# A mixture-of-experts kernel: the gate weights move into the spare columns of the context chunks, and the early loads are merged

## The reference, cut to what matters

```python
x = x + tanh(g_xattn) * (gelu(layernorm(x) @ ctx.T) @ ctx)      # per batch, ctx is 375 x 256
n = layernorm(x)
top1 = argmax(n @ gate_w.T + gate_b)                            # 8 experts
x = x + tanh(g_ffn) * (relu(n @ w1[top1].T + b1[top1]) @ w2[top1].T + b2[top1])
```

## Time and profile before

| what | value |
|---|---|
| median of 3 runs | 111.12 us (110.9 to 111.33) |
| profiled execution, its time | 111.79 us |
| profiled execution, its span | 110.0 us |
| busy share of the span: TensorE | 92% |
| VectorE, ScalarE, GpSimd | 49%, 26%, 36% |
| mean DMA rate over the span | 258 GB/s |
| read from HBM | 26.33 MB |

### The profile page before, as it was taken

The page is one execution under the profiler, slowest core; times in us unless marked ns, Lnnn a source line. Parts: engine busy times, 40 slices in busy tenths (PEclk is TensorE's granted clock), DMA queues, the critical chain, the costliest instruction groups (busy, mean ns, idle before and its releaser), DMA issues.

```text
span 110.0 us, 2150 instructions
## 1 busy us (share of the span) xinstructions
PE 100.7 (92%) x704; PEld 92.7 (84%) x705; DVE 53.5 (49%) x204; ACT 28.6 (26%) x91; POOL 39.9 (36%) x97
## 2 busy tenths in 40 slices
PE   5999899999999997799999999999999999999900
PEld 5998669999988895799989999899999998998600
DVE  0461578669689884796555332344133241333010
ACT  5616143212351440152302303223032140220000
POOL 3276386353664937700330557030030030300330
PEclk9999999999999999999999999999999999999996
DMA  3999999999995202599999999999992010010101
GB/s 80 316 331 246 404 419 422 404 427 426 413 414 202 86 0 65 128 352 359 368 416 402 419 420 365 415 426 426 432 419 114 7 44 0 0 40 6 46 19 35
DMA packets 6734, 28.36 MB, mean 258 GB/s; under 512 B 1149, under 2 KB 2511, under 8 KB 4672
## 3 DMA queue, kind: packets, MB, share of 16 engines
q1 hardware_dynamic: 4688, 25.09, 58.2%
q0 software_dynamic: 864, 2.12, 6.3%
q10 hardware_dynamic: 1168, 0.98, 2.8%
HBM read 26.33 MB, written 2.11 MB: 259 GB/s over the span
## 4 chain that ended last, share of the span: by engine, by line
PE 71%; DMA 11%; DVE 6%; issue 3%; POOL 2%; SPq 2%; ACTq 0%; ACT 0%; POOLq 0%; DVEq 0%
PE bank L978 29%; PE bank L987 26%; DMA x<-in_x_rest 8%; PE bank L928 6%; PE bank L910 5%; DMA region<-x_rows,from_row 3%; PE bank L960 2%; PE bank L919 2%; DVE x L582 1%; SPq L241 1%; PE bank L900 1%; POOL out_rows L386 1%; DVE stats L589 1%; SPq L231 1%; DVE region L791 1%
## 5 line engine op out<-in xcount | busy, mean ns | idle before, releaser
L978 PE MATMUL bank<-region,w 128*128 128x128 f32 x288 | 34.7, 277 | 0.3 <-ACT region L485 0.3
L978 PEld LDWEIGHTS bank<-region,w 128*128 128x128 f32 x288 | 33.8, 192 | 0.8 <-ACT region L485 0.4
L987 PE MATMUL bank<-w,region 128*128 128x256 f32 x144 | 32.6, 379 | 0.0
L987 PEld LDWEIGHTS bank<-w,region 128*128 128x128 f32 x144 | 26.7, 190 | 3.2
L520 ACT ACTIVATE region<-bank,smalls 128x128 f32<-128x128 f32 x40 | 12.5, 363 | 39.9 <-PE bank L978 38.5
L386 POOL DMA_INDIRECT out_rows<-region,to_row x9 | 8.9, 989 | 33.9 <-DVE region L813 32.4
L797 DVE TENSOR_SCALAR region<-bank,smalls 128x128 f32<-128x128 f32 x32 | 9.7, 346 | 13.8 <-PE bank L978 13.4
L381 POOL DMA_INDIRECT region<-x_rows,from_row x9 | 9.3, 1032 | 15.7 <-DMA region<-x_rows,from_row 12.2
L813 DVE SCALAR_TENSOR_TENSOR region<-bank,tg,region 128x256 f32<-128x256 f32 (+1 forms) x9 | 4.4, 484 | 19.0 <-PE bank L987 19.0
L910 PEld LDWEIGHTS bank<-xnT,region 128*125 128x125 f32 x96 | 11.4, 188 | 2.2 <-issue 1.6
L910 PE MATMUL bank<-xnT,region 128*125 128x120 f32 x96 | 12.0, 275 | 0.8 <-issue 0.7
(11 more groups left out here) (118 smaller groups left out, 85.7 us busy)
## 6 DMA issues: line engine op xcount, KB each, us to landing
w<-in_w1t SPq DMA_DIRECT2D x8, 1024.0 KB, 23.3
w<-in_w2t SPq DMA_DIRECT2D x8, 1024.0 KB, 26.5
region<-in_ctx SPq DMA_DIRECT2D x5, 771.0 KB, 13.2
region<-in_ctx SPq DMA_DIRECT2D x3, 396.0 KB, 9.1
region<-in_ctx SPq DMA_DIRECT2D x3, 375.0 KB, 4.2
x_rows<-x ACTq DMA_DIRECT2D x8, 113.8 KB, 6.4
b2b<-in_b SPq DMA_DIRECT2D x1, 896.0 KB
x<-in_x_rest SPq DMA_DIRECT2D x1, 586.2 KB, 8.3
```

The lines of the kernel that those rows point to most:

```text
L978: mm = pe.matmul(hT_ps[k][:, part % 2 * P:(part % 2 + 1) * P], w1[:, e, n * H + part * P:n * H + (part + 1) * P], xgT[:, j % 2, n * P:(n + ...
L987: mm = pe.matmul(y[:, 0:D], hidT[:, q, part, :], w2[:, e, part * D:(part + 1) * D], start=(part == 0), stop=(part == KH - 1))
```

## The change

The gate weights leave `x_logits`. A chunk of context has 125 rows for 128 positions; its transposed form now gets 128 columns, and the three spare ones of each chunk hold gate weights, so the scores give x times gate weights in the output rows 125 to 127. ScalarE copies the last 32 output rows without gelu (`spare_rows`) before the gelu of the first 125 overwrites those of them that are context rows. The context rows get 8 more columns, with ones in the spare rows only, so `attend` carries the values past the gelu into columns 264 to 271. `x_share` therefore reads its input from attend's output. For the last batch VectorE does that itself in two small instructions (`add_last_logits`). `xnT` moves into the space of the last expert's w2. Contexts 0 and 1 come in two pieces (transposed, rows), x of batches 2 to 7 in one, contexts 2 to 7 whole, and w2 of expert 1 is loaded after SP's wait.

```diff
-DL = D + E
-CW = KD * CTX + CC * DL
+SPARE = P - CR
+CT = KD * CC * P
+DL = D + 2 * E
+CW = CT + CC * DL
...
-HEAD = 3
+HEAD = 2
...
-            load_x(0).then_inc(x_in[0], 16)
-            load_context_T(0)
-            load_x(1).then_inc(x_in[1], 16)
-            load_context_T(1)
-            load_x(2).then_inc(x_in[2], 16)
-            load_context_rows(0)
-            sp.dma_start(x2[0:S, HEAD:B, :], x_rest).then_inc(x_in[3], 16)
-            load_context_T(2)
-            load_context_rows(1)
-            load_context_rows(2)
-            for b in range(3, B):
-                load_context(b)
+            for b in range(HEAD):
+                load_x(b).then_inc(x_in[b], 16)
+            sp.dma_start(pair_T, ctx_pair[:, 0:HEAD * CT]).then_inc(pair_T_in, 16)
+            sp.dma_start(x2[0:S, HEAD:B, :], x_rest).then_inc(x_in[HEAD], 16)
+            sp.dma_start(pair, ctx_pair[:, HEAD * CT:HEAD * CW]).then_inc(pair_in, 16)
+            for b in range(HEAD, B):
+                sp.dma_start(cxs[:, b, :], ctx[b - HEAD]).then_inc(cx_in[b - HEAD], 16)
 
             load_expert(0)
             sp.dma_start(b2b[:, 0:D], b2[0:D].partition_broadcast(P)).then_inc(b2_in[0], 16)
-            load_expert(1)
+            sp.dma_start(w1[:, 1, :], w1t[1]).then_inc(w1_in[1], 16)
...
-            load_expert(2)
+            sp.dma_start(w2[:, 1, :], w2t[1]).then_inc(w2_in[1], 16)
             sp.dma_start(b2b[:, D:E * D], b2[D:E * D].partition_broadcast(P)).then_inc(b2_in[1], 16)
-            for e in range(3, E):
+            for e in range(2, E):
                 load_expert(e)
...
-            def gelu(b):
-                scored = sc_ps[b % 2][0:CR, 0:CC * SL].rearrange("p (c n) -> p c n", c=CC)
+            def spare_rows(b):
+                scored = sc_ps[b % 2][P - 32:P, 0:CC * SL].rearrange("p (c n) -> p c n", c=CC)
                 act.wait_ge(sc_done, b + 1)
                 if b >= 2:
                     act.wait_ge(at_done, b - 1)
+                act.activation(gel[P - 32:P, b % 2, :].rearrange("p (c n) -> p c n", c=CC), scored[:, :, 0:S],
+                               ACT.Copy).then_inc(spare_ok, 1)
...
             def x_share(b):
-                act.wait_ge(lg_done, b + 1)
+                act.wait_ge(at_done, b + 1)
                 act.wait_ge(std_ok, b + 1)
-                act.activation(x2[0:S, b, RAW:ROW + E], at_ps[b % 2][0:S, DL:DL + E], ACT.Copy,
+                act.activation(x2[0:S, b, RAW:ROW + E], at_ps[b % 2][0:S, D + E:DL], ACT.Copy,
                                scale=mv[0:S, b, 4:5]).then_inc(xl_ok, 1)
...
             for b in range(B):
                 if b + 1 < B:
-                    gelu(b + 1)
-                    x_share(b + 1)
+                    spare_rows(b + 1)
                 if b + 2 < B:
                     xnT_copy(b + 2)
                 if b + 1 < B:
+                    gelu(b + 1)
                     gate_share(b + 1)
+                    x_share(b)
...
+            def add_last_logits():
+                b = B - 1
+                dve.wait_ge(std_ok, B)
+                dve.tensor_scalar(x2[0:S, b, RAW:ROW + E], at_ps[b % 2][0:S, D + E:DL], mv[0:S, b, 4:5], None,
+                                  ALU.mult).then_inc(xl_ok, 1)
+                dve.wait_ge(xl_ok, B)
+                dve.scalar_tensor_tensor(out=x2[0:S, b, RAW:ROW + E], in0=at_ps[b % 2][0:S, D:D + E], scalar=tg[0:S, 0:1],
+                                         in1=x2[0:S, b, RAW:ROW + E], op0=ALU.mult, op1=ALU.add).then_inc(last_l_ok, 1)
...
+            add_last_logits()
             route(6, 1, 5)
             rank_one(5, 3)
             route(7, 1, 6)
...
                 if b >= 2:
                     pe.wait_ge(cg_ok, b - 1)
                 for c in range(CC):
                     for k in range(KD):
-                        mm = pe.matmul(sc_ps[b % 2][0:CR, c * SL:(c + 1) * SL],
-                                       cxT[:, b, k * CTX + c * CR:k * CTX + (c + 1) * CR],
+                        mm = pe.matmul(sc_ps[b % 2][:, c * SL:(c + 1) * SL],
+                                       context_T(b)[:, (k * CC + c) * P:(k * CC + c + 1) * P],
                                        xnT[:, b % 2, k * SL:(k + 1) * SL], start=(k == 0), stop=(k == KD - 1))
                 mm.then_inc(sc_done, 1)
-
-            def x_logits(b):
-                if b >= 2:
-                    pe.wait_ge(x2_ok, b - 1)
-                for k in range(KD):
-                    mm = pe.matmul(at_ps[b % 2][0:S, DL:DL + E], xnT[:, b % 2, k * SL:k * SL + S],
-                                   xnT[:, b % 2, k * SL + S:(k + 1) * SL], start=(k == 0), stop=(k == KD - 1))
-                mm.then_inc(lg_done, 1)
...
             scores(0)
             turn_xn(1)
-            x_logits(0)
+            keep_warm(2)
             pe.wait_ge(gwc_ok, 2)
```

More of the change, by code:

```diff
@@ L54, with gated_cross_attention_moe @@
 NOWHERE = 65536.0
-def gated_cross_attention_moe(nc, x, x_rest, ctx, small, w1t, w2t, b2, out):
+def gated_cross_attention_moe(nc, x, x_rest, ctx_pair, ctx, small, w1t, w2t, b2, out):
     x2_dram = nc.dram_tensor("x2_rows", (TOKENS, ROW), F32, kind="Internal").ap()
@@ L95, in gated_cross_attention_moe @@
         x2 = sb("x2", [P, B, ROW + E])
-        xnT = sb("xnT", [P, 2, KD * SL])
+        xnT = w2[:, E - 1, H:H + 2 * KD * SL].rearrange("p (q n) -> p q n", q=2)
         g_mean = sb("g_mean", [P, P])
@@ L174, in ranks, with context_T, context_rows @@
             return {3: banks[6], 6: banks[1], B - 1: banks[6]}.get(b, rk_ps)
-        x_in = [sem("x_in0"), sem("x_in1"), sem("x_in2"), sem("x_in3")]
+        def context_T(b):
+            if b < HEAD:
+                return pair_T[:, b * CT:(b + 1) * CT]
+            return cxs[:, b, 0:CT]
+        def context_rows(b):
+            if b < HEAD:
+                return pair[:, b * CC * DL:(b + 1) * CC * DL]
+            return cxs[:, b, CT:CW]
+        x_in = [sem("x_in0"), sem("x_in1"), sem("x_in2")]
         small_in, b2_in = sem("small_in"), [sem("b2_in0"), sem("b2_in1")]
-        cxT_in = [sem("cxT_in0"), sem("cxT_in1"), sem("cxT_in2")]
-        cx_in = [sem(f"cx_in{b}") for b in range(B)]
+        pair_T_in, pair_in = sem("pair_T_in"), sem("pair_in")
+        cx_in = [sem(f"cx_in{b}") for b in range(HEAD, B)]
         w1_in = [sem(f"w1_in{e}") for e in range(E)]
@@ L904, in scores @@
                 pe.wait_ge(xnT_ok, b + 1)
-                pe.wait_ge(cxT_in[b] if b < 3 else cx_in[b], 16)
+                pe.wait_ge(pair_T_in if b < HEAD else cx_in[b - HEAD], 16)
                 if b >= 2:
@@ L1144 @@
     from concourse.bass_utils import run_bass_kernel_spmd
+    ctx = np.asarray(ctx_1024)
+    gate_w = np.pad(np.asarray(L0_ffn_gate_w).reshape(E, KD, P).transpose(1, 2, 0), ((0, 0), (0, 0), (0, CC * SPARE - E)))
+    ctx_T = np.concatenate([ctx.transpose(0, 2, 1).reshape(B, KD, P, CC, CR),
+                            np.broadcast_to(gate_w.reshape(KD, P, CC, SPARE), (B, KD, P, CC, SPARE))], axis=4)
+    ctx_T = ctx_T.transpose(0, 2, 1, 3, 4).reshape(B, P, CT)
+    ctx_rows = np.zeros((B, P, CC, DL), ctx.dtype)
+    ctx_rows[:, 0:CR, :, 0:D] = ctx.reshape(B, CC, CR, D).transpose(0, 2, 1, 3)
+    for e in range(E):
+        ctx_rows[:, CR + e % SPARE, e // SPARE, D + E + e] = 1
+    ctx_rows = ctx_rows.reshape(B, P, CC * DL)
     arrays = {
```

45 lines of the change are left out of this document (22 added, 23 removed).

## The result

The changed kernel takes **116.4 us** (median of 4, 115.3 to 116.77) where the kernel before takes 111.22 in the same comparison: a ratio of **1.044** [1.036, 1.053]. The forecast was 111.7, range 109.8 to 112.9: wrong, and outside the range. The profiled execution took 115.3 with a span of 113.6 us, 3.6 more than the 110.0 of before. The other three executions took 116.15 to 116.77, with spans of 114.4 to 114.9 and mean granted clocks of 0.966 to 0.971 where the profiled one has 0.976; so what follows on its trace accounts for 3.6 us of span. About 1 us more goes with a lower clock in the executions without a trace; that the clock is its cause is inferred.

The account below looks back on a forecast made before the run. TensorE bounds it to attention 5, VectorE until the gather, then TensorE again. Attention 5 -0.1, add 5 +0.3, last logits +0.4, behind the gather 0: +0.6, put at 111.7 us from the 111.12 median; range 109.8 to 112.9.

Parts of the forecast that it names:

- The loads: Early load queue: batch 2's whole context is the gate, its scores start at 14.4 us, bounds 12.6 and 14.8.
- T2: Start of scores 2, once batch 2's whole context has landed: forecast 14.4 us, nothing else ending later before it.
- Rival D: TensorE's clock falls after idling between scores 1 and about 12.4 us: some +1.5, 113.2 us; chance 0.05.
- Behind the gather: Late weight loads: expert 2's w1 lands at 57.1, TensorE wants it at 57.50; priced at 0, upper bound 0.7.
- Rival C: Expert 2's w1 comes late, so TensorE waits 0.7 before up(3): 112.4 us; chance 0.13.
- The logits path: Per-batch TensorE work and added waits: x logits go (-0.30 each), while add 5 gains +0.3 and last logits +0.4.
- Four x logits: TensorE's x logits matmuls, 0.30 per batch, disappear: a gain of 1.0 over four batches.
- the rank-sum wait: TensorE waits for POOL's second running count before the rank sums of batches 0 to 2: +0.4, bounds 0.2 and 0.6.
- the x share: ScalarE's scaled copy now follows attention, and VectorE's residual add waits for it: +0.30 on every add.
- the last logits: Two more VectorE instructions before route(6) for the last batch: +0.40, bounds 0.3 to 0.5.
- The period: TensorE's time per batch up to attention 5: from 3.19 to 2.94 us.
- my two signs of being wrong: The prediction is wrong if scores 2 start before 13.6, or if TensorE waits before up(3).

Follow-up runs that it names:

- e5: The changed kernel with 12 warming matmul calls instead of 1 ahead of scores 0: 114.55 us, ratio 1.030.
- g1: The changed kernel with the merged transposed pair issued between x of batch 0 and x of batch 1: 113.95 us, ratio 1.023.
- e6: The changed kernel with the transposed pair loaded in two pieces, one per batch, at the same place in the queue: 117.18 us, ratio 1.058.
- e1: The changed kernel with the late order of the weights' loads put back as in the kernel before: 113.57 us, ratio 1.023.
- f1: The changed kernel with expert 2's w1 issued first in the late group, ahead of expert 1's w2 and the biases: 114.32 us, ratio 1.026.
- e3: The changed kernel with early pieces and late order both put back, leaving only the new logits path: 111.89 us, ratio 1.006.
- f2: The changed kernel with the transposed pair and the pair's rows each in a contiguous DRAM array of its own: 114.81 us, ratio 1.033.
- h2: The changed kernel with only two orders changed: merged pair ahead of x of batch 1, expert 2's w1 ahead of expert 1's w2: 111.97 us, ratio 1.005.
- e4: The kernel before with only the merged early pieces in the changed order: 113.56 us, ratio 1.021.
- g2: The changed kernel with the transposed pair in halves, ordered x 0, half 0, x 1, half 1: 115.71 us.
- h1: The changed kernel with merged pair before x of batch 1, old late loads, rank sums behind attention 5, last x share through ScalarE: 110.37 us, ratio 0.993.

## Why the prediction was wrong

**The loads** is the step that failed first. It forecast T2, the start of scores 2, at 14.4, by counting bytes along a curve up to the piece that batch 2 needs, and said that before T2 nothing else ends later. Scores 2 began at 15.69, and three things ended at about that time. Batch 2's own context landed at 15.4, 0.6 beyond my slow bound of 14.8. x_rest landed at 11.8 where I had 10.4, so batch 2's transposes could begin at 13.8 and not at 12.6; e5, with the clock kept and x_rest at 12.2, has scores 2 at 16.05. And a merged piece is ready when all of it has landed: scores 0, which had waited for 375 KB in the second place of the queue, now waited for 768 KB in the third. They began at 8.94 instead of 6.45, at half pace, and I worked out T2 without asking when they could begin. Behind all three are slower loads: 242 GB/s from 3 to 9 us, with the hole of 125 from 3 to 4, which no byte curve of the kernel before holds. With one issue swapped (g1) the same bytes moved at 317, the context landed at 12.9 and scores 2 began at 13.66, earlier than my 14.4. So a curve read in one order of the queue missed by 1.0 on one side and by 1.5 on the other.

**Rival D** (the clock falls) came true with a chance of 0.05, and from another wait than I named: not behind scores 1 but in front of scores 0. The doubling behind its price holds (scores 0 took 2.69 for 1.33), though the opening matmuls from which I took it had a granted clock of 1.00 in the rows. What the fall costs in the end differs: nearly nothing in the profiled execution, 1.85 between the medians of e5 and the changed kernel, 2.6 to 4.0 between the executions of e6. I rated it low because no row showed idle time of over 1.2 us; that was absence of evidence, and the forecast itself lengthened such waits.

**Behind the gather** failed too. I scaled the landing to 57.1, which with the measured shift of 2.0 is 59.1; it was 60.8. I counted 12.1 (5.3 + 6.8) from the first late issue; it took 13.55 (47.25 to 60.8), as w1 was itself issued 0.85 behind that and landed 12.7 later. The other 0.27 is that SP began this group 2.27 later and not 2.0. Rival C named the mechanism and priced it at 0.7; it cost 1.34 of wait and 0.24 of slower up(3), and e1 and f1 take it away. I priced at zero what by my own numbers had 0.4 us of cover, behind two bounds that differed by 1.0.

**The logits path** held. Four x logits gave 1.16, the rank-sum wait was real (0.69 against 0.4, just beyond its bound of 0.6), the x share 0.36 against 0.30, the last logits 0.33 against 0.40. The period is 2.90 against 2.94. The kernel in which only this part is left measures +0.6 in 100, 111.89 us, against my 111.7. That is near by luck in part, since my sum began from merged loads (attention 5 ends at 29.6), and e3 has the old ones (29.08). Of my two signs of being wrong one came (TensorE waits before up(3)); the other, scores 2 before 13.6, looked to the wrong side. I also read the stretch from 29.75 to 39.31 as VectorE's alone; in the kernel before, TensorE ends the chain from 35.93 to 39.28. The last logits cost their 0.33 all the same.

What stays open is why two x pieces issued one behind the other at the head of the queue leave the loads at a third to a half of their rate a microsecond later.

## What to carry to other kernels

When pieces are merged, ask of each consumer which whole piece it now waits for and what stands ahead of it in the queue, the first consumer above all; a sum of bytes to a later consumer doesn't see it. A rate read in one order of the queue doesn't carry over to another. An idle time of TensorE that a load opens has a second price, the clock, paid in some executions only: look at more than the one with a trace. And a load with under a microsecond to spare is a term of the sum, not a zero.

## What the runs showed of the hardware

Loads from 3 to 4 us moved 88 to 137 GB/s with the two 112 KB x pieces at the head of the queue (8 traces) and 264 to 360 with a context piece between them (10 traces).

Of the traces, the clock fell behind an idle time of TensorE of 1.71 (f2), 1.87 (h2), 2.10 (e1), 2.20 (e4), 2.39 (g2), 2.48 (the changed kernel) and 2.79 us (f1). It stayed at 1.00 behind 1.23 (h1), 1.26 (e5) and once behind 2.74 (e6). So the length of the idle time alone doesn't decide it.

An earlier start of the first scores didn't make the kernel faster (e6, 1.058 against 1.044, with intervals that overlap): it moved the idle time behind scores 1, and the executions of that one kernel spread from 114.48 to 118.47 us.
